# A recurrent cell in six layers: tokens made the stationary operand, gates used as gathered, the gated product turned

## The reference

```
def _L0_rec_ref(state, token, ih, hh):      # state (1024, 256), ih (6, 4000, 256), hh (6, 256, 256)
    for i in range(6):
        gate = ih[i][token]
        state = jnp.tanh(state + jnp.matmul(state, hh[i]) * gate)
    return state
```

## Time and profile before

| | |
|---|---|
| runs | 68.02, 68.29, 68.86 us; median 68.29 |
| profiled execution, span from first to last instruction | 66.9 us |
| instructions | 1118 |
| mean granted TensorE clock | 0.974 of full speed |
| DMA | 10.03 MB, 39.2% of the 16 engines' time in the gathers' queue, 17.9% in SyncE's |
| idle before the step of L336 (turns), ended by a gather's landing | 4.1 us |
| idle before GpSimd's L198, ended by ScalarE's tanh | 8.0 us |

### The profile page before, as it was taken

How to read it: one execution, slowest core, us unless ns; L and a number is a source line. 1 busy time by engine, 2 the same in 40 slices (tenths; PEclk the granted TensorE clock), 3 DMA queues, 4 the chain that set the end, 5 groups by cost and what they waited for, 6 DMA issues and landing times.

```text
span 66.9 us, 1118 instructions
## 1 busy us (share of the span) xinstructions
PE 53.4 (80%) x402; PEld 50.1 (75%) x402; DVE 50.7 (76%) x73; ACT 43.5 (65%) x80; POOL 41.0 (61%) x40
## 2 busy tenths in 40 slices
PE   0996896667359999999999699996799987999100
PEld 0993886464329999998999599995799977999000
DVE  0306850803863899999999999999999999999920
ACT  5217633019255996899991789944899748986440
POOL 4088876846788659679898697998724307263000
PEclk9999999999975799999999999999999999999999
DMA  0679979698888989988476480463620000003463
GB/s 0 115 244 333 331 147 173 156 278 172 167 175 262 202 183 228 247 237 268 170 176 147 105 181 37 130 167 96 159 76 0 0 10 0 0 0 137 147 220 124
DMA packets 5893, 10.03 MB, mean 150 GB/s; under 512 B 768, under 2 KB 4352, under 8 KB 5888
## 3 DMA queue, kind: packets, MB, share of 16 engines
q0 software_dynamic: 1920, 6.29, 39.2%
q1 hardware_dynamic: 3968, 3.68, 17.9%
HBM read 8.92 MB, written 1.05 MB: 149 GB/s over the span
## 4 chain that ended last, share of the span: by engine, by line
DVE 45%; issue 22%; DMA 14%; POOL 10%; ACT 2%; PE 2%; DVEq 0%
DVE pre L298 19%; DVE pre L307 12%; DMA gate<-gates_dram,row_of 12%; POOL gate L176 10%; DVE wl L279 9%; DVE sl L282 3%; DMA tok<-token_dram 3%; PE turned L336 2%; ACT s L262 1%; DVE pre L316 1%; ACT gate_t L218 1%; DVE pre L319 1%; DVE wrap L272 0%; DVE tok_held L270 0%; DVE row_of L274 0%
## 5 line engine op out<-in xcount | busy, mean ns | idle before, releaser
L176 POOL DMA_INDIRECT gate<-gates_dram,row_of x24 | 25.3, 1054 | 8.0 <-issue 5.8
L359 PE MATMUL prod<-sh,wh 128*128 128x256 f32 x96 | 21.6, 307 | 0.5 <-ACT wh L206 0.5
L359 PE MATMUL prod<-sl,wh 128*128 128x256 f32 x96 | 20.1, 291 | 2.1 <-DVE sl L282 2.1
L298 DVE TENSOR_TENSOR pre<-prod,gate_t 128x512 f32<-128x512 f32 x23 | 15.7, 683 | 6.3 <-ACT gate_t L218 3.9
L359 PE MATMUL prod<-sh,wl 128*128 128x256 f32 x96 | 19.8, 288 | 0.3 <-DVE wl L279 0.3
L336 PE MATMUL turned<-ident,gate 128*128 128x128 f32 x96 | 15.8, 283 | 4.2 <-DMA gate<-gates_dram,row_of 4.1
L307 DVE TENSOR_TENSOR pre<-pre,s 128x512 f32<-128x512 f32 x23 | 17.8, 773 | 0.4
L198 POOL TENSOR_TENSOR sl<-s,sh 128x512 fp32r<-128x512 f32 x8 | 12.4, 1551 | 8.4 <-ACT s L228 8.0
L359 PEld LDWEIGHTS prod<-sl,wh 128*128 128x128 f32 x96 | 15.0, 193 | 2.8 <-DVE sl L282 2.7
L227 ACT ACTIVATE sh<-pre 128x512 fp32r<-128x512 f32 x20 | 12.6, 632 | 6.6 <-DVE pre L307 5.9
L218 ACT COPY gate_t<-turned 128x512 f32<-128x512 f32 x24 | 13.6, 574 | 4.6 <-PE turned L336 4.6
(11 more groups left out here) (13 smaller groups left out, 5.0 us busy)
## 6 DMA issues: line engine op xcount, KB each, us to landing
w<-hh_dram SPq DMA_DIRECT2D x6, 256.0 KB
s<-state_t_dram SPq DMA_DIRECT2D x4, 256.0 KB
out_t_dram<-s SPq DMA_DIRECT2D x3, 256.0 KB, 2.1
gate<-gates_dram,row_of POOLq DMA_INDIRECT x24, 4.3
out_t_dram<-s SPq DMA_DIRECT2D x2, 128.0 KB, 1.9
tok<-token_dram SPq DMA_DIRECT2D x1, 4.0 KB, 1.7
```

The costliest lines, as they stand in the source:

```text
L176: nc.gpsimd.indirect_dma_start(gate[h][:, t], None, gate_rows[h], bass.IndirectOffsetOnAxis(row_of[:, t:t + 1].bitcast(u32), 0),).then_inc ...
L298: nc.vector.tensor_tensor(pre[:, q], prod[q][:, :, :], gate_t[:, n], ALU.mult).then_inc(gated, 1)
L359: last = nc.tensor.matmul(bank[:, m, :], a[:, l, c, m * P:(m + 1) * P], b[:, q, c, :], start=(i == 0 and c == 0), stop=(i == 2 and c == KC ...
```

## The change

The twelve matmuls of a product have their operands exchanged: the state of 128 tokens (`sh` or `sl`) is stationary, and the weights (`wh`, `wl`; 256 columns) move. The product comes out with tokens on the partitions, as the gathered gates lie. VectorE multiplies it by the gates as gathered into a new tile `gp` (`gating`), TensorE turns that (`turn(n)`, four transposes into `turned[q]`), and VectorE adds the state to what was turned, from PSUM (`sum_up`). ScalarE's copy of the gates is gone. The passes of a product are ordered anew: all eight matmuls with `sh` first, then the four with `sl`.

The gates come in two parts, of two and four layers: eight gathers of 2 KB rows and eight of 4 KB rows. GpSimd issues the first eight, then four of the large ones, and the last four behind the state subtractions of steps 4 to 7, one each. GpSimd makes the low part of the state in all of the steps 4 to 19; VectorE keeps those of the input and of steps 0 to 3 and all weight subtractions. The weights of layer 1 are loaded behind the second gather instead of the first.

```diff
-PART_LAYERS = [2, 2, 2]
+PART_LAYERS = [2, 4]
...
-WEIGHTS_AFTER = {1: (0, 0), 2: (0, 5), 3: (1, 0), 4: (1, 2), 5: (1, 4)}
-POOL_LOW_STATE = [5, 7, 9, 11, 13, 15, 17, 19]
-POOL_LOW_WEIGHTS = [1, 2]
+WEIGHTS_AFTER = {1: (0, 1), 2: (0, 5), 3: (1, 0), 4: (1, 2), 5: (1, 4)}
+POOL_LOW_STATE = list(range(4, LAST_LAYER))
+DVE_LOW_STATE = [0, 1, 2, 3]
+LOW_WEIGHTS_BEHIND = {0: 1, 5: 2, 9: 3, 13: 4, 17: 5}
...
             def _(pool):
...
+                pool.wait_ge(rows_ready, 1)
+                for t in range(TILES):
+                    gather(0, t)
+                for t in range(4):
+                    gather(1, t)
+                for n in POOL_LOW_STATE:
+                    low_state(n)
+                    if n < 2 * QUARTERS:
+                        gather(1, n)
...
             def _(act):
...
                 round_weights(1)
...
+                for n in range(STEPS - 1):
                     tanh(n)
+                    l, q = divmod(n, QUARTERS)
+                    if q == 0 and l + 2 < LAYERS:
+                        round_weights(l + 2)
...
             def _(dve):
...
+                def gating(n):
+                    q = n % QUARTERS
+                    h, gates = gates_of(n, range(TPQ))
+                    dve.wait_ge(prod_ready, n + 1)
+                    for t in range(TPQ):
+                        dve.wait_ge(gate_in[h][q * TPQ + t], 16)
+                    nc.vector.tensor_tensor(gp[:, q], prod[q][:, :, :], gates, ALU.mult).then_inc(gated, 1)
+
+                def sum_up(n):
+                    q = n % QUARTERS
+                    dve.wait_ge(turn_ready, n + 1)
+                    nc.vector.tensor_tensor(pre[:, q], turned[q][:, :, :], s[:, q], ALU.add).then_inc(pre_ready, 1)
...
                 for n in range(STEPS - 1):
...
+                    gating(n)
+                    if n in LOW_WEIGHTS_BEHIND:
+                        low_weights(LOW_WEIGHTS_BEHIND[n])
+                    if n - 3 in DVE_LOW_STATE:
+                        dve.wait_ge(s_ready, n - 2)
+                        low_state((n - 3) % QUARTERS)
+                    if n > 0:
+                        sum_up(n - 1)
...
             def _(pe):
+                def high(n, tiles, banks):
+                    l, q = divmod(n, QUARTERS)
+                    for half in (wh, wl):
+                        if half is wl:
+                            pe.wait_ge(wl_ready, l + 1)
+                        for t in tiles:
+                            for c in range(KC):
+                                nc.tensor.matmul(banks[t][:, t, :], sh[:, q, c, t * P:(t + 1) * P], half[:, l, c, :],
...
+                def low(n, tiles, banks):
+                    l, q = divmod(n, QUARTERS)
+                    wait_sl(pe, n)
+                    for t in tiles:
                         for c in range(KC):
+                            last = nc.tensor.matmul(banks[t][:, t, :], sl[:, q, c, t * P:(t + 1) * P], wh[:, l, c, :],
...
+                def turn(n):
+                    pe.wait_ge(gated, n + 1)
+                    turns(n, range(TPQ), [turned[n % QUARTERS]] * TPQ)
...
                 product(0)
                 product(1)
+                product(2)
+                product(3)
                 turn(0)
                 turn(1)
+                product(4)
                 turn(2)
+                product(5)
                 turn(3)
                 turn(4)
+                for n in range(6, STEPS - 1):
                     product(n)
+                    turn(n - 1)
```

More of the change, by code:

```diff
@@ L171, in _, with gather, low_state @@
                                         base=0, pattern=[[-1, P]], channel_multiplier=1).then_inc(ident_ready, 1)
[L173 to L193, removed]
+                def gather(h, t):
+                    nc.gpsimd.indirect_dma_start(
+                        gate[h][:, t], None, gate_rows[h],
+                        bass.IndirectOffsetOnAxis(row_of[:, t:t + 1].bitcast(u32), 0),
+                    ).then_inc(gate_in[h][t], 16)
+                def low_state(n):
                     q = n % QUARTERS
@@ L321, in _ @@
             @block.tensor
             def _(pe):
-                def turn(k):
-                    n = TURN_ORDER[k]
+                def high(n, tiles, banks):
                     l, q = divmod(n, QUARTERS)
-                    h = max(h for h in range(PARTS) if FIRST_LAYER[h] <= l)
-                    if k >= GATE_BANKS:
-                        pe.wait_ge(gate_ready, k - GATE_BANKS + 1)
-                    for t in range(TPQ):
-                        tile = q * TPQ + t
-                        pe.wait_ge(gate_in[h][tile], 16)
-                        for c in range(KC):
-                            at = (l - FIRST_LAYER[h]) * HIDDEN + c * P
-                            last = nc.tensor.transpose(turned[k % GATE_BANKS][:, c, t * P:(t + 1) * P],
-                                                       gate[h][:, tile, at:at + P], ident[:, :])
-                    last.then_inc(gate_turned, 1)
+                    for half in (wh, wl):
[4 more added lines that the diff above has]
+                                nc.tensor.matmul(banks[t][:, t, :], sh[:, q, c, t * P:(t + 1) * P], half[:, l, c, :],
+                                                 start=half is wh and c == 0 and t == tiles[0], stop=False,
+                                                 skip_group_check=True)
@@ new lines, in low, with turns @@
+                def low(n, tiles, banks):
+                    l, q = divmod(n, QUARTERS)
+                    wait_sl(pe, n)
+                    for t in tiles:
+                        for c in range(KC):
+                            last = nc.tensor.matmul(banks[t][:, t, :], sl[:, q, c, t * P:(t + 1) * P], wh[:, l, c, :],
+                                                    start=False, stop=c == KC - 1, skip_group_check=True)
+                    last.then_inc(prod_ready, 1)
+                def turns(n, tiles, banks):
+                    q = n % QUARTERS
+                    for t in tiles:
+                        for c in range(KC):
+                            last = nc.tensor.transpose(banks[t][:, c, t * P:(t + 1) * P],
+                                                       gp[:, q, t, c * P:(c + 1) * P], ident[:, :])
+                    last.then_inc(turn_ready, 1)
@@ L346, in product @@
                     pe.wait_ge(sh_ready, n + 1)
-                    for m in range(KC):
-                        bank = prod[q] if n < STEPS - 1 else last_prod[m]
-                        if n == STEPS - 1 and m == 1:
-                            pe.wait_ge(gated, LAST_LAYER + 1)
-                        passes = [(wh, sh), (wl, sh), (wh, sl)]
-                        for i, (a, b) in enumerate(passes):
-                            if m == 0 and i == 1:
-                                wait_wl(pe, l)
-                            if m == 0 and i == 2:
-                                wait_sl(pe, n)
-                            for c in range(KC):
-                                last = nc.tensor.matmul(bank[:, m, :], a[:, l, c, m * P:(m + 1) * P], b[:, q, c, :],
-                                                        start=(i == 0 and c == 0), stop=(i == 2 and c == KC - 1))
-                        if m == KC - 1 or n == STEPS - 1:
-                            last.then_inc(prod_ready, 1)
+                    high(n, range(TPQ), [prod[q]] * TPQ)
+                    low(n, range(TPQ), [prod[q]] * TPQ)
                 pe.wait_ge(ident_ready, 1)
```

127 lines of the change are left out of this document (46 added, 81 removed).

## The result

The changed kernel took **78.45 us** (median; 77.77 to 79.60) against 68.58 for the kernel before beside it (68.02 to 69.39): a ratio of **1.142, 95% interval 1.131 to 1.154**. The forecast was 73.1 with a range of 69.8 to 75.8: right in sign, too small by 5.35 us, and outside its range. The profiled execution took 78.06 us, its span is 76.2.

What follows compares the result with a forecast made beforehand. Gathers bound the first 20 us, VectorE from about 24. Product 13 at 46.3 (5.6 us lost), ten steps (18.7) to 65.0, stretches to 65.4, end 69.3, store 2.4: span 71.7; plus 1.4: 73.1 us, range 69.8 to 75.8.

Steps and rivals of the forecast that it cites:

- What bounds the kernel before: Gathers bind the first 20 us; VectorE from about 24 us to the end, at 2.19 us a step.
- the relief of VectorE: VectorE in steady state: 6.6 us a layer instead of 8.74, the new sums never waiting for GpSimd.
- the new pace: Where nothing is late, TensorE is the new bound at 1.87 us a step, 0.32 below before.
- the 0.4 us that I added for the last two: Weight subtractions of layers 4 and 5 run beside GpSimd: 0.4 us for both.
- The mechanism: GpSimd's subtraction and gather pairs issue the last gather at 40.0; it lands at 45.0, gating 11 waits, 5.6 us lost.
- case C: Worse rival, 0.12: gather instruction goes by bytes, 76.9 us at most, or landing takes 7.2 us, 75.1.
- Start: First steps: layer 1's weights in ScalarE at 16.3, product 8 starting at 31.3, GpSimd's subtraction 4 at 30.4.
- string of exchanges: From gating 3 at 20.0 to tanh 4 at 30.3, two engines in strict order; VectorE's order binds, not TensorE.
- From product 13: From 46.3 us TensorE binds: ten steps, 18.7 us, product 23 at 65.0.
- GpSimd's pace alone: Of the 5.6 us lost before product 13, 2.5 would be lost to GpSimd's pace without late gathers.
- A: Rival, 0.15: GpSimd is late but the gates are not; only its pace counts, 2.9 us less, 70.2.
- B: Rival, 0.13: GpSimd keeps up and VectorE's relief shows; 67.1 us, or 62.8 if low parts 0 to 3 come in time.

Runs made afterwards that it cites:

- e12: e9 with gathers 13 and 14 issued behind subtraction 0 and 15 and 16 behind subtraction 1, not one each behind 0 to 3: 68.0 us, ratio 0.986.
- e1: The changed kernel with all sixteen gathers issued before GpSimd's first state subtraction: 72.8 us, ratio 1.067.
- e8: The changed kernel with GpSimd waiting before gather 9 until the sixth gather has landed: 76.1 us, ratio 1.115.
- e2: The changed kernel with the weights of layers 1 and 2 loaded right behind the states, waiting for no gather: 77.8 us, ratio 1.138.
- e3: The changed kernel with the edits of e1 and e2 together: 73.7 us (69.65 to 76.19).
- e9: e5 with the weights of layers 3, 4 and 5 issued behind earlier gathers: 67.0 us, ratio 0.976.
- e5: e3 with the low parts of steps 0 to 3 on GpSimd instead of VectorE, gathers 13 to 16 one each behind them: 68.0 us.
- e7: e5 with 57 idle transposes on TensorE between products 3 and 4: 68.7 us, ratio 0.996.

## Why the prediction was right in sign and wrong in size

*What bounds the kernel before, the relief of VectorE, the new pace.* Right. The sums take 0.683 us in the mean of 23 and 0.69 at most, in a kernel with sixteen GpSimd subtractions; products follow at 1.87 us. Of the six weight subtractions one stretched, to 1.35 us; the 0.4 us that I added for the last two was not needed (nine steps in 16.8).

The rule taken from the Trainium skill (SBUF — State Buffer, "Who interferes with whom") is borne out on both sides by these rows: no sum with a PSUM input was stretched, the one weight subtraction that met a GpSimd subtraction (39.56 against 39.06) was, and e12's took 2.96 us beside two of them.

*GpSimd.* The mechanism was right and close in size: pairs of 2.44 to 2.69 us (forecast 2.7), last gather issued 9.1 us after subtraction 4 (forecast 9.6), landing 5.3 us later (forecast 5.0), VectorE idle 4.25 us before gating 11 (forecast 4 to 5). The instruction took 0.95 us for 4 KB rows as for 2 KB ones, so case C did not come by that road. e1 shows its worth, 5.7 us.

*Start: the step that failed.* Subtraction 4 started at 34.11 instead of **30.4**, and these 3.7 us went through to the end. Most of it is one term. The prediction put the first weights into ScalarE at 16.3 ("I take 16.3 (15 to 17)"); it was 19.17. The load was issued 2.4 us later than before, at 10.89, where the prediction says "about 2 us" and adds 1.4; and from issue to rounding it took 8.3 us, where it had taken 6.4 (8.47 to 14.87) and I counted on no more. VectorE cannot go on without it, and through its order it makes the gating of step 3 late:
```profile
23.00 0.68 DVE L235 TENSOR_TENSOR gp<-prod,gate 128x512 f32<-128x512 f32 x1
...
26.03 0.69 DVE L240 TENSOR_TENSOR pre<-turned,s 128x512 f32<-128x512 f32 x1 [1.75 <-PE turned L295]
...
29.75 0.69 DVE L240 TENSOR_TENSOR pre<-turned,s 128x512 f32<-128x512 f32 x1 [1.27 <-PE turned L295]
```
The sum had that gating at 20.0, bound by the last tile of gates. The tile landed at 21.1 and so was 1.1 us late itself, but the gating started only at 23.00, 3.0 us late; sum 2 (26.03) is then 2.9 late and sum 3 (29.75) 3.75. Why the first load took longer is not shown: the pause of e8 did not shorten it.

The rest, some 0.7 us, is a term that the sum leaves out. Its string of exchanges was written for two engines in strict order, VectorE and TensorE. There is a third: the rounding of the second weights stands before tanh 1 on ScalarE. It held tanh 1 until 26.60 and product 5 until 27.37. Here the cause is shown by e8: the gathers went into the queues without a pause, and the second load met them. In moving a subtraction from GpSimd to VectorE I counted its time on VectorE and not the wait that GpSimd lost. From gating 3 to subtraction 4 the string takes 11.1 us in the changed kernel and 10.35 in e8, where the second weights are on time; the prediction had 10.4. So the string itself was sized about right.

And e2 and e3 say that early weights do not finish it. Without any late weight of layers 1 and 2 the string through VectorE's low parts is still there (e3: product 8 at 36.24; e2: 11.0 us from gating 3 at 21.97 to subtraction 4 at 32.95). The two waits run side by side, and the later one decides.

*From product 13.* It came 0.2 us later behind gating 11 than in the sum, and then the low clock, 3.0 us instead of 1.87 for that step: 1.1 us that the prediction had no term for, though it foresaw TensorE idling at this very place.

*Sum.* Start 3.7, pairs -0.5, landing 0.3, signals 0.2, clock 1.1, no stretched subtractions -0.4, tail -0.1: 4.3 of the 4.5 us of span. The other 0.85 us of the miss is the offset to the median: I took 1.4 us from a median and a profile of different executions; here 78.06 of the profiled run stand 1.9 above its span, and the median 0.4 above that. Some of the prediction's additions are off by a little, without any weight: its own lower end comes to 71.1 and not 71.3, case C's late landing to 75.3 and not 75.1, and GpSimd's pace alone to 2.7 us and not 2.5.

*Rivals.* A asked for faster landing and B for subtraction 4 five us earlier; neither came by itself. B is what e9 makes of the change by hand: product 8 at 29.63, from there fifteen steps in 28.6 us (15 times 1.87 is 28.05), span 64.4.

## What to carry to other kernels

When work is moved off an engine, write down also the waits that it made there: they may have spaced the transfers behind it, and how long a load takes to land depends on the queue that it meets (3.0 or 8.6 us here). In each engine's written order, look for an instruction that waits for data of a later stage in front of one that an earlier stage needs: in e5 a rounding for layer 3 held a tanh of layer 1 for 3.6 us, and taking that wait away went together with 1.0 us less in the medians (e9). And when an edit that removes a visible wait brings nothing, try it together with the next wait in the same stretch before giving up either: here two edits worth 0 and 0.5 us were worth 6.5 together.

## What the runs showed of the hardware

- Weight loads of 256 KB each took 3.0 us (e8, a short queue of gathers), 8.6 (after) and 11.0 (e9, issued in the middle of them) from issue to landing. The Trainium skill (DMA: Bandwidth & Descriptors, "SWDGE vs HWDGE vs iDMA") has the two kinds of queue share each engine in turn; the rows agree that the load is slowed and not stopped, and no run here separates turns from mere load.
- With the DMA engines 96 to 103% busy, gathers of 2 KB rows moved 179 GB/s with all else in the stretch, those of 6 KB rows 420 GB/s. The instruction on GpSimd took mostly 0.95 us, for 128 rows of 2, 4 or 6 KB.
- Idle transposes held the granted clock at 1.00 from 15 to 30 us, where it was 0.77 without them, and the kernel was no faster (e7, e5).
- A VectorE subtraction with both inputs in SBUF took 0.68 to 0.72 us with no GpSimd subtraction beside it, 1.35 us beside one (after) and 2.96 us beside two in a row (e12); 23 sums with one input in PSUM took 0.68 to 0.69.
